# Two-layer model on one core: keys, values and router of layer 1 in three equal pieces, and products summed over tokens on DVE

## Chip, cores and metric

The program runs on one core of one Trainium2 chip. The metric is the device time in microseconds (us) of one execution of the whole program; of the kernel before there are three runs without a profiler, and one profiled execution.

## The reference

Two layers, each an attention part and a feed-forward part, over 4096 tokens of 512 numbers. This change is in the attention part of layer 1, which is no softmax attention: keys and values of a token are normed and multiplied number by number, and these products are summed over the 2048 tokens of a batch (the kernel has two batches). The second part cut out below is the router whose logits are made beside them.

```python
Xn = _layernorm(X, gamma, beta)
QKV = Xn @ W_in + b_in
Q, K, V = jnp.split(QKV, 3, axis=-1)
K = _rotary(K, ROT_DIM)
V = _rotary(V, ROT_DIM)
A = jnp.sum(_cos_sim(K) * _cos_sim(V), axis=-2)
A = (1.0 - IDENTITY_WEIGHT) * A + IDENTITY_WEIGHT
Y = A[:, None, :] * Q
Y = Y @ W_out + b_out
return Y + X
...
logits = x.astype(jnp.float32) @ router_weight.astype(jnp.float32).T
```

The last line is the router of layer 1; the kernel makes these logits (`logits1`, 8 columns) from the same transposed tile as keys and values. `axis=-2` is the axis of the tokens.

## The kernel before

The program is a row of stages, each with its own instruction streams for the five engines: front, attention, experts, the combining stage (`phase_mix`), and the last stage (`phase_last`). Engines are tied together by semaphores only; each runs its stream in the order in which it is written.

`phase_mix` runs from about 2350 to 3115 us. Its tokens are cut in 8 groups (`GROUPS`) of 4 tiles (`GT`) of 128 tokens, so 32 tiles, 16 for each batch. An outer loop has 10 iterations of 18 steps (`STEPS`). In iteration `it` the first 8 iterations do the shared expert of layer 0 for group `it`: in every step PE has twelve matmuls of 512 columns (`gate_up`, into `b_psG` or `b_psU`, or `down_of`, into `b_psY`). Between them stands the work on the groups before: a group `n` has a clock `rel`, which is `k` in iteration `n + 1` and `k + 18` in iteration `n + 2`. In iterations 8 and 9 only that work is left, and PE has nothing of its own to do between the pieces. This stretch, from 3016 us on, is called the stage's end here.

For group `n`: at `rel` 2 to 7 DVE adds up the layer's output (`sums`, `residual`) and works out the norm (`variance`, `deviation`). Tile `j` of the group then has its turn from `rel = 8 + 4 j`: PE transposes the normed tile into the PSUM bank `psX` (`turn`), ACT and DVE make of it the upper and the lower half of `c_xT` (`x_upper`, `x_lower`); two steps later PE does `router` (twelve matmuls of 8 columns into a corner of `psX`) and `keys(t, 0)` (twelve of 512 columns into `psK`), one step later `keys(t, 1)`. Twelve are three for each of the four chunks of 128 rows: `mm3` multiplies upper by lower, lower by upper, and upper by upper half. DVE takes each piece out of PSUM (line 2130 for the logits, line 2040 for `c_kv`), and PE's next piece into the same bank waits for that (`kv_ready`). One step later POOL turns keys and values by the table and multiplies them into `c_prod` (`rotate`, six operations), and ACT sums their squares. At `rel` 25 and 26 DVE makes the group's factors `rn` of them. At `rel` 29 PE does `similar`: sixteen fp32 matmuls of one column (they show as 32 in the trace), products as the stationary side and `rn` as the moving one, whose result (4 columns, in `psX`) DVE copies to `aparts` (line 2140). The last stage sums `aparts` over the four groups of a batch.

DVE's order inside a step matters: first the expert's product or half, then the group one iteration back, then the group two back. So the fourth tile of a group (`rel` 20 to 24, steps 2 to 6 of an iteration) meets the next group's `sums` and `residual` on DVE (steps 2 to 4), and stands behind them.

Of the kernel before, what the change touches and what calls it, by code (L numbers as in the profile page):

```python
# [20 lines left out]
P = 128  # L21
# [1456 lines left out]
def phase_mix(nc, env):  # L1478
# [13 lines left out]
    A_AT = 29  # L1492
    with ctx:
# [14 lines left out]
        wr = [sb(f"c_wr{h}", [P, KC, NROUTED], F32R) for h in range(2)]  # L1508
# [8 lines left out]
        rs = rsb[:, 0, :].rearrange("p (a i o) -> p a i o", a=2, o=2)  # L1517
        n2 = [sb(f"c_n2{i}", [P, GT, 2]) for i in range(2)]
# [16 lines left out]
        psL = psX[:, 0, 0:NROUTED]  # L1535
        psA = psX[:, 0, NROUTED:NROUTED + KC]
# [16 lines left out]
        rot, prod_ready, a_full, a_used = sem("c_rot"), sem("c_prod"), sem("c_a_full"), sem("c_a_used")  # L1553
        wr_in, wr_hi, wr_split = sem("c_wr_in"), sem("c_wr_hi"), sem("c_wr_split")
# [91 lines left out]
        def _(pool):  # L1646
            def rotate(t):
# [16 lines left out]
                if t >= GT:  # L1664

                    pool.wait_ge(a_full, t // GT)
# [36 lines left out]
        def _(pe):  # L1703
# [29 lines left out]
            def turn(t):  # L1733
# [6 lines left out]
                if t % GT == 1 and t > GT:  # L1740

                    pe.wait_ge(a_used, t // GT)
# [59 lines left out]
            for g, k, after in steps():  # L1802
# [9 lines left out]
                for n, rel in after:  # L1812
                    if (t := tile_at(n, rel, XS)) is not None:
                        turn(t)
                    if (t := tile_at(n, rel, XS + 2)) is not None:
                        router(t)
# [3 lines left out]
                    if rel == A_AT:  # L1820
                        similar(n)

        @block.scalar
        def _(act):
# [69 lines left out]
            def fold_upper(c):  # L1894
                act.wait_ge(centred, 2 * KC + c + 1)
                act.activation(env.wkv1[0][:, c, :, :], w[c][:, 1:3, :], ACT.Copy).then_inc(i_hi, 1)
# [5 lines left out]
            act.activation(wr[0][:, :, :], wr_raw[:, :, :], ACT.Copy).then_inc(wr_hi, 1)  # L1902
# [41 lines left out]
        def _(dve):  # L1944
# [85 lines left out]

            def keys(t, a):
                dve.wait_ge(k_full, 2 * t + a + 1)
                if t == a == 0:
                    dve.wait_ge(b_out, 3)
                if a == 0 and t % GT == 0:
                    dve.wait_ge(r2_ready, t // GT + 1)
                if a == 0 and t >= 2:
                    dve.wait_ge(prod_ready, t - 1)
                    dve.wait_ge(sq_ready, t - 1)
                dve.scalar_tensor_tensor(kv[t % 2][:, a, :], psK[:, :], env.stat[:, t, 2:3], env.bkv[:, a, :],  # L2040
                                         ALU.mult, ALU.add).then_inc(kv_ready, 1)
# [649 lines left out]
```

## Time and profile before

| what | us |
|---|---|
| runs without a profiler, median of 3 | 4430.65 (4429.25 to 4431.05) |
| profiled execution, first to last instruction | 4443.7 |
| PE busy (matmuls) | 4139.1, 93% |
| DVE busy | 2115.4, 48% |
| ACT busy | 1662.0, 37% |
| POOL busy | 1352.3, 30% |

The profiled execution is the one whose trace is read here. Its own time is the span of 4443.7 us; no other time of it is recorded, and it is 13 us longer than the median of the runs without a profiler. Busy shares are of the whole span.

### The profile page before, as it was taken

To read this page: it belongs to the slowest core of one execution; us is meant where nothing else is said; L and a number is where in the kernel's file an instruction comes from. 1 tells how busy PE (TensorE), PEld (TensorE's weight loads), DVE (VectorE), ACT (ScalarE), POOL (GpSimd) and SP (SyncE) were. 2 spreads that over 40 slices of the span, in tenths; PEclk is the share of its full clock that TensorE was granted. 3 is DMA by queue.
4 is the path that set the end of the run, shared out by engine and by line. 5 is a ranking of instruction groups with operands and counts; after the bars stand their busy time and mean duration, and the time that the engine had idled before them with its cause. 6 is when DMAs were issued, how large, how long until landed. Compare 5 with 4: busy or idle time off the path is not lost. (4 is left out here: it accounts for less than half of the span.)

```text
span 4443.7 us, 69429 instructions
## 1 busy us (share of the span) xinstructions
PE 4139.1 (93%) x23045; PEld 3550.2 (80%) x23046; DVE 2115.4 (48%) x4125; ACT 1662.0 (37%) x3234; POOL 1352.3 (30%) x2020
## 2 busy tenths in 40 slices
PE   6975999899999999999997999997899999999998
PEld 5864777689889999989985777785688888788887
DVE  4447888744444444444435445543343333333333
ACT  2214777634334444443433333331332222222222
POOL 0002454455555555555551333334000000000000
PEclk9877999999999999999998999997999999999999
DMA  5767787455556556555645444431432331231321
GB/s 189 282 239 192 137 162 143 97 136 123 113 120 129 128 124 136 121 128 117 154 75 181 152 140 145 154 105 50 152 107 71 100 102 60 100 102 60 102 81 45
DMA packets 351912, 561.41 MB, mean 126 GB/s; under 512 B 33089, under 2 KB 198625, under 8 KB 347490
## 3 DMA queue, kind: packets, MB, share of 16 engines
q1 hardware_dynamic: 282770, 394.19, 29.8%
q0 software_dynamic: 68944, 164.62, 17.3%
q8 instruction: 120, 1.97, 0.2%
q14 instruction: 78, 0.64, 0.1%
HBM read 384.36 MB, written 174.34 MB: 126 GB/s over the span
## 5 line engine op out<-in xcount | busy, mean ns | idle before, releaser
L1250 POOL DMA_INDIRECT acc_d<-e_yw,e_to x208 | 335.9, 1615 | 287.0 <-ACT e_yw L1407 270.4
L2310 POOL DMA_DIRECT2D out<-d_res x32 | 17.3, 542 | 1305.3 <-DVE d_res L2542 1305.3
L2489 DVE TENSOR_TENSOR d_h<-d_sg,d_psU 128x512 f32<-128x512 f32 x144 | 99.1, 688 | 521.3 <-PE d_psU L107 462.9
L983 ACT ACTIVATE a_pr<-a_sm,a_nmax 128x272 f32<-128x272 f32 x512 | 263.8, 516 | 124.9 <-DVE a_nmax L1037 120.7
L105 PE MATMUL e_psG<-e_gu,e_xT 128*128 128x352 f32 x832 | 290.6, 349 | 10.0 <-DVE e_xT L1461 9.2
L1469 DVE TENSOR_TENSOR e_h<-e_sg,e_psU 128x352 f32<-128x352 f32 x208 | 108.3, 521 | 396.4 <-ACT e_sg L1420 393.8
L107 PE MATMUL e_psG<-e_gu,e_xT 128*128 128x352 f32 x832 | 272.5, 327 | 0.0
L106 PE MATMUL e_psG<-e_gu,e_xT 128*128 128x352 f32 x832 | 272.3, 327 | 0.0
L105 PE MATMUL e_psU<-e_gu,e_xT 128*128 128x352 f32 x832 | 270.9, 326 | 0.0
L106 PE MATMUL e_psU<-e_gu,e_xT 128*128 128x352 f32 x832 | 269.5, 324 | 0.0
L105 PE MATMUL e_psY<-e_wd,e_hT 128*128 128x512 f32 (+1 forms) x624 | 265.7, 426 | 1.2 <-DVE e_hT L1452 1.2
L107 PE MATMUL e_psU<-e_gu,e_xT 128*128 128x352 f32 x832 | 266.4, 320 | 0.0
L1220 POOL DMA_INDIRECT e_xs<-xn_d,e_idx x209 | 209.9, 1004 | 174.4 <-POOL e_idx L1217 168.4
L2417 ACT ACTIVATE d_hT<-d_h 128x512 fp32r<-128x512 f32 x144 | 91.0, 632 | 459.6 <-DVE d_h L2489 401.6
L1037 DVE CUSTOM_DVE_ANT_0 a_sm<-a_psS,a_mask 128x272 f32<-128x272 f32 x512 | 214.2, 437 | 82.5 <-PE a_psS L877 54.4
L1420 ACT ACTIVATE e_sg<-e_psG 128x352 f32<-128x352 f32 x208 | 96.4, 463 | 409.5 <-PE e_psU L107 409.5
L107 PE MATMUL e_psY<-e_wd,e_hT 128*128 128x512 f32 (+1 forms) x624 | 247.1, 396 | 0.0
L106 PE MATMUL e_psY<-e_wd,e_hT 128*128 128x512 f32 (+1 forms) x624 | 245.4, 393 | 0.0
L2411 ACT ACTIVATE d_sg<-d_psG 128x512 f32<-128x512 f32 x144 | 86.0, 598 | 423.5 <-PE d_psG L107 423.4
L1401 ACT ACTIVATE e_hT<-e_psH 128x384 fp32r<-128x384 f32 x208 | 102.2, 491 | 372.6 <-PE e_psH L1340 372.6
L105 PE MATMUL d_psG<-d_x,d_gu 128*128 128x512 f32 x576 | 225.4, 391 | 12.7 <-DMA d_x<-xT_d 12.7
L105 PE MATMUL d_psU<-d_x,d_gu 128*128 128x512 f32 x576 | 227.8, 395 | 0.0
(430 smaller groups left out, 12004.9 us busy)
## 6 DMA issues: line engine op xcount, KB each, us to landing
d_gu_raw<-in_wgu SPq DMA_DIRECT2D x144, 512.0 KB, 3.3
qk_d<-f_qk SPq DMA_DIRECT2D x32, 1024.0 KB, 6.5
a_q<-qk_d SPq DMA_DIRECT2D x96, 256.0 KB
a_k<-qk_d SPq DMA_DIRECT2D x96, 256.0 KB, 4.7
e_rawgu<-in_w_gate SPq DMA_DIRECT2D x32, 704.0 KB, 5.9
e_rawgu<-in_w_up SPq DMA_DIRECT2D x32, 704.0 KB, 5.8
b_gu_raw<-in_wgu SPq DMA_DIRECT2D x40, 512.0 KB, 3.8
xT_d<-f_xT SPq DMA_DIRECT2D x16, 1024.0 KB, 14.3
```

Of the source, the lines that this page charges most:

```text
L105: pe.matmul(out, lhs[0], rhs[1], start=first, stop=False, **kw)
L106: pe.matmul(out, lhs[1], rhs[0], start=False, stop=False, **kw)
L107: return pe.matmul(out, lhs[0], rhs[0], start=False, stop=last, **kw)
L983: act.activation(pr[half][:, h % HH, :], sm[s % SR][:, :], ACT.Exp, bias=nmax[s % SR][:, :], scale=-1.0, accum_out=rs[u % 2][:, h:h + 1]). ...
L1037: dve.tensor_tensor_reduce(out=sm[s % SR][:, :], in0=psS[s % SR][:, PERSIST:2 * KW], in1=m[:, :], scale=-SCALE, scalar=3.0e38, op0=ALU.add ...
L1220: pool.indirect_dma_start(rows[:, :], None, env.xn_d, bass.IndirectOffsetOnAxis(ap=idx[k][:, :].bitcast(U32), axis=0))\
L1250: pool.indirect_dma_start(env.acc_d, bass.IndirectOffsetOnAxis(ap=to[:, :].bitcast(U32), axis=0), yw[:, :], None, compute_op=ALU.add).then ...
L1401: act.activation(hT[0][:, :, :], psH[:, :, :], ACT.Copy).then_inc(hT_hi, 1)
L1420: act.activation(sg[:, :], psG[:, 0:M], ACT.Silu).then_inc(sg_ready, 1)
L1469: dve.tensor_tensor(hv[:, :], sg[:, :], psU[:, 0:M], ALU.mult).then_inc(h_ready, 1)
L2417: act.activation(h2[q % 2][0][:, :], hv[q % 2][:, :], ACT.Copy).then_inc(h_hi, 1)
L2489: ins = dve.tensor_tensor(hv[q % 2][:, :], sg[q % 2][:, :], psU[:, :], ALU.mult)
```

## The change

Keys, values and router have 512 + 512 + 8 = 1032 columns. They are put side by side in one tensor (`wkv1`, 1032 columns for each chunk) and cut in three pieces of 344 (`CW`). The third piece (336 columns of values and the 8 of the router) comes first and goes into the whole bank `psX` (`last_keys`), the others into `psK` as before. DVE takes out three pieces of 336 or 344 columns where it took two of 512, and the logits as before.

The sum over tokens is moved: DVE adds the weighed products of each tile into one tile `simacc` (`add`, at `rel` 27 to 30), and PE turns this into a column once per batch with a column of ones, four matmuls in place of sixteen for each group (`similar`, at `rel` 31 of every fourth group, into `psK`). POOL's wait before it writes `c_prod` again is now for `added`, no longer for `a_full`. The sum over groups in the last stage falls away.

```diff
-    A_AT = 29
+    GB = GROUPS // B
+    ADD_AT = 27
+    A_AT = ADD_AT + GT
+    CW = (2 * D + NROUTED) // 3
...
+        simacc = rsb[:, 1, :]
...
-        psL = psX[:, 0, 0:NROUTED]
-        psA = psX[:, 0, NROUTED:NROUTED + KC]
+        psXf = psX[:, :, :].rearrange("p c k -> p (c k)")
+        psL = psXf[:, CW - NROUTED:CW]
+        psA = psK[:, 0:KC]
...
-                    pool.wait_ge(a_full, t // GT)
+                    pool.wait_ge(added, t - GT + 1)
...
-                if t % GT == 1 and t > GT:
-
-                    pe.wait_ge(a_used, t // GT)
...
-            def router(t):
+            def columns(t, out, a):
+
+                for c in range(KC):
+                    ins = mm3(pe, out, [xT[t % 2][h][:, c, :] for h in range(2)],
+                              [env.wkv1[h][:, c, a * CW:(a + 1) * CW] for h in range(2)], c == 0, c == KC - 1)
+                return ins
+
+            def last_keys(t):
                 pe.wait_ge(x_split, t + 1)
                 if t == 0:
                     pe.wait_ge(wr_split, 1)
-                for c in range(KC):
-                    ins = mm3(pe, psL, [xT[t % 2][h][:, c, :] for h in range(2)], [wr[h][:, c, :] for h in range(2)],
-                              c == 0, c == KC - 1)
-                ins.then_inc(l_full, 1)
+                    pe.wait_ge(i_split, KC)
+                columns(t, psXf[:, 0:CW], 2).then_inc(l_full, 1)
 
             def keys(t, a):
                 if t or a:
                     pe.wait_ge(kv_ready, 2 * t + a)
-                else:
-                    pe.wait_ge(i_split, KC)
+                if t == GT * GB + 1 and a == 0:
+
+                    pe.wait_ge(a_used, 1)
+                columns(t, psK[:, 0:CW], a).then_inc(k_full, 1)
+
+            def similar(b):
+                pe.wait_ge(added, GT * GB * (b + 1))
+
+                pe.wait_ge(kv_ready, 2 * min(GT * GB * (b + 1) + 1, TILES))
                 for c in range(KC):
-                    ins = mm3(pe, psK[:, :], [xT[t % 2][h][:, c, :] for h in range(2)],
-                              [env.wkv1[h][:, c, a, :] for h in range(2)], c == 0, c == KC - 1)
-                ins.then_inc(k_full, 1)
...
-                for c in range(KC):
-                    for j in range(GT):
-                        ins = pe.matmul(psA[:, c:c + 1], prod[:, j, c * P:(c + 1) * P], rn[g % 2][:, j:j + 1],
-                                        start=j == 0, stop=j == GT - 1)
+                    ins = pe.matmul(psA[:, c:c + 1], simacc[:, c * P:(c + 1) * P], ones[:, 0:1],
+                                    start=True, stop=True)
                 ins.then_inc(a_full, 1)
...
+            def last_keys(t):
+                dve.wait_ge(l_full, t + 1)
+                if t == 0:
+                    dve.wait_ge(b_out, 3)
+                if t % GT == 0:
+                    dve.wait_ge(r2_ready, t // GT + 1)
+                if t >= 2:
+                    dve.wait_ge(prod_ready, t - 1)
+                    dve.wait_ge(sq_ready, t - 1)
+                dve.tensor_copy(env.logits1[:, t, :], psL)
+                scaled(t, psXf[:, 0:CW - NROUTED], 2 * CW, 2 * D).then_inc(l_used, 1)
...
+            def add(t):
+                g, j = divmod(t, GT)
+                dve.wait_ge(rn_ready, g + 1)
+                dve.wait_ge(prod_ready, t + 1)
+                if t % (GT * GB) == 0:
+                    if t:
+                        dve.wait_ge(a_full, g // GB)
+                    dve.tensor_scalar(simacc[:, :], prod[:, j, :], rn[g % 2][:, j:j + 1], None, ALU.mult)\
+                       .then_inc(added, 1)
+                    return
+                dve.wait_ge(added, t)
+                dve.scalar_tensor_tensor(simacc[:, :], prod[:, j, :], rn[g % 2][:, j:j + 1], simacc[:, :],
+                                         ALU.mult, ALU.add).then_inc(added, 1)
```

The first place is DVE's stream at the fourth tile of a group, behind `residual` of the next group (`c_s`, `c_x`, `c_st`). Before:

```order
L1985 TENSOR_TENSOR c_s<-c_s,c_acc 128x512
L1987 TENSOR_TENSOR c_x<-c_s,c_x 128x512
L1989 BN_STATS c_st<-c_x 128x6
L2130 COPY logits<-c_psX 128x8
L2040 SCALAR_TENSOR_TENSOR c_kv<-c_psK,stat,bkv 128x512
L1970 TENSOR_TENSOR b_hT<-b_h,b_hT 128x512
L1950 TENSOR_TENSOR b_gu<-b_gu_raw,b_gu 128x1024
```

With the change one more operation stands there before PE's bank `psK` is free:

```order
L1991 TENSOR_TENSOR c_x<-c_s,c_x 128x512
L1993 BN_STATS c_st<-c_x 128x6
L2050 COPY logits<-c_psX 128x8
L2037 SCALAR_TENSOR_TENSOR c_kv<-c_psX,stat,bkv 128x336
L2037 SCALAR_TENSOR_TENSOR c_kv<-c_psK,stat,bkv 128x344
L1974 TENSOR_TENSOR b_hT<-b_h,b_hT 128x512
L1954 TENSOR_TENSOR b_gu<-b_gu_raw,b_gu 128x1024
```

The two pieces of 512 columns have become three, of which two lie side by side here.

The second place is also on DVE, in steps 8 to 12 of an iteration, where the group two back gives its factors `c_rn` (first row) and, with the change, its products are added into `c_rs`. With the change:

```order
L2012 TENSOR_TENSOR c_rn<-c_rn,c_tmp_n 128x4
L2064 TENSOR_SCALAR c_rs<-c_prod,c_rn 128x512
L1969 TENSOR_TENSOR b_h<-b_sg,b_psU 128x512
L2050 COPY logits<-c_psX 128x8
L2037 SCALAR_TENSOR_TENSOR c_kv<-c_psX,stat,bkv 128x336
L2037 SCALAR_TENSOR_TENSOR c_kv<-c_psK,stat,bkv 128x344
L2068 SCALAR_TENSOR_TENSOR c_rs<-c_prod,c_rn,c_rs 128x512
L1974 TENSOR_TENSOR b_hT<-b_h,b_hT 128x512
L1954 TENSOR_TENSOR b_gu<-b_gu_raw,b_gu 128x512
L2037 SCALAR_TENSOR_TENSOR c_kv<-c_psK,stat,bkv 128x344
L2068 SCALAR_TENSOR_TENSOR c_rs<-c_prod,c_rn,c_rs 128x512
L2032 TENSOR_TENSOR c_xT<-c_psX,c_xT 128x512
```

Before, no `c_rs` row was there, and in step 11 DVE's copy of the column (line 2140) waited for PE. The three shown here and a fourth in step 12 stand among the pieces of the tile whose turn it is.

The third place is on PE, at the end of `keys(t, 1)` in step 11 of the iteration (`c_psK` is the piece, `b_psG` the expert's next matmuls). Before:

```order
L105 MATMUL c_psK<-wkv,c_xT 128x512
L106 MATMUL c_psK<-wkv,c_xT 128x512
L107 MATMUL c_psK<-wkv,c_xT 128x512
L1773 MATMUL c_psX<-c_rn,c_prod 128x1 x16
L105 MATMUL b_psG<-b_x,b_gu 128x512
L106 MATMUL b_psG<-b_x,b_gu 128x512
```

With the change:

```order
L105 MATMUL c_psK<-wkv,c_xT 128x344
L106 MATMUL c_psK<-wkv,c_xT 128x344
L107 MATMUL c_psK<-wkv,c_xT 128x344
L105 MATMUL b_psG<-b_x,b_gu 128x512
L106 MATMUL b_psG<-b_x,b_gu 128x512
```

The sixteen one-column matmuls are gone from here, in all eight groups; four of them per batch come back at `rel` 31.

## Rows read from the trace of the kernel before

**Rows 1.** The page's head
```profile
span 4443.7 us, 69429 instructions
```

**Rows 2.** Windows: stretch; length; busy PE, PEld, DVE, ACT, POOL; PEclk; DMA
```profile
2543.00:2630.70 87.70, 86.14 (x409) 70.08 (x408) 43.27 (x76) 30.27 (x53) 31.24 (x37) 0.96 0.41 141
...
2630.70:2716.90 86.20, 84.63 (x409) 68.73 (x408) 43.30 (x76) 30.27 (x53) 31.24 (x37) 0.98 0.42 144
...
3016.30:3114.10 97.80, 69.09 (x277) 55.82 (x276) 33.99 (x70) 17.65 (x42) 41.20 (x51) 0.75 0.13 49
...
2545.50:2552.30 6.80, 6.80 (x22) 5.74 (x23) 0.16 (x1) 0.00 (x0) 4.56 (x6) 0.50 0.09 39
```

**Rows 3.** Timeline of PE, one tile: start, length, instruction
```profile
2644.56 0.17 PE L105 MATMUL c_psX<-c_wr,c_xT 128*128 128x8 f32 x1
...
2645.82 0.47 PE L105 MATMUL c_psK<-wkv,c_xT 128*128 128x512 f32 x1
...
2648.69 0.39 PE L105 MATMUL b_psG<-b_x,b_gu 128*64 128x512 f32 x1
...
2651.46 0.40 PE L105 MATMUL c_psK<-wkv,c_xT 128*128 128x512 f32 x1
...
2654.25 0.39 PE L105 MATMUL b_psU<-b_x,b_gu 128*64 128x512 f32 x1
```

**Rows 4.** Timeline of PE in the experts' stage, pieces of 352 columns
```profile
1499.78 0.32 PE L106 MATMUL e_psG<-e_gu,e_xT 128*128 128x352 f32 x1
...
1502.85 0.32 PE L107 MATMUL e_psU<-e_gu,e_xT 128*128 128x352 f32 x1
```

**Rows 5.** Timeline of PE, the products summed over tokens
```profile
2542.96 4.55 PE L1773 MATMUL c_psX<-c_rn,c_prod 128*128 128x1 f32 x32
...
2630.73 3.66 PE L1773 MATMUL c_psX<-c_rn,c_prod 128*128 128x1 f32 x32
...
2634.25 0.78 PE L105 MATMUL b_psG<-b_x,b_gu 128*128 128x512 f32 x1
```

**Rows 6.** Groups by form, DVE: busy us, mean ns, idle before
```profile
L2040 DVE SCALAR_TENSOR_TENSOR c_kv<-c_psK,stat,bkv 128x512 f32<-128x512 f32 x64 | 48.0, 750 | 171.7 <-PE c_psK L107 171.7
...
L2058 DVE SCALAR_TENSOR_TENSOR c_acc<-c_rs,i_beta,c_acc 128x1536 f32<-128x1536 f32 x1 | 1.8, 1821 | 0.1
```

**Rows 7.** Waits of PE, 2430 to 3010 us
```profile
PE c_psK L105 <- DVE c_kv L2040: 9.4, 6, 1.6
```

**Rows 8.** Timeline around the wait for a tile's keys
```profile
2603.19 0.15 DVE L2130 COPY logits<-c_psX 128x8 f32<-128x8 f32 x1
...
2604.05 0.50 PE L105 MATMUL c_psK<-wkv,c_xT 128*128 128x512 f32 x1 [1.56 <-DVE c_kv L2040]
```

**Rows 9.** Waits, timeline and window of PE in the experts' stage
```profile
PE e_psH L1340 <- DVE e_h L1469: 10.2, 5, 2.3
...
1200.83 0.90 PE L1340 MATMUL e_psH<-ident,e_h 128*128 128x128 f32 x3 [2.09 <-DVE e_h L1469]
...
1200.60:1204.00 3.40, 3.17 (x12) 3.05 (x13) 1.93 (x4) 1.21 (x2) 1.71 (x4) 0.50 0.38 66
```

**Rows 10.** Timeline of the stage's end
```profile
3063.74 0.37 PE L105 MATMUL c_psX<-c_wr,c_xT 128*128 128x8 f32 x1 [1.41 <-DVE c_xT L2028]
...
3066.32 0.77 PE L105 MATMUL c_psK<-wkv,c_xT 128*128 128x512 f32 x1
...
3072.37 0.50 PE L105 MATMUL c_psK<-wkv,c_xT 128*128 128x512 f32 x1 [0.84 <-DVE c_kv L2040]
...
3106.96 6.98 PE L1773 MATMUL c_psX<-c_rn,c_prod 128*128 128x1 f32 x32 [6.54 <-POOL c_prod L1669]
...
3113.98 0.16 DVE L2140 COPY aparts<-c_psX 128x4 f32<-128x4 f32 x1 [7.74 <-PE c_psX L1773]
```

**Rows 11.** Timeline of DVE, one operation twice
```profile
2587.90 2.32 DVE L1950 TENSOR_TENSOR b_gu<-b_gu_raw,b_gu 128x1024 fp32r<-128x1024 f32 x1
...
2604.51 1.22 DVE L1950 TENSOR_TENSOR b_gu<-b_gu_raw,b_gu 128x1024 fp32r<-128x1024 f32 x1
```

More of the change, by code:

```diff
@@ L1507, in phase_mix @@
         xT = [[sb(f"c_xT{i}{h}", [P, KC, P], F32R) for h in range(2)] for i in range(2)]
-        wr = [sb(f"c_wr{h}", [P, KC, NROUTED], F32R) for h in range(2)]
         wr_raw = sb("c_wr_raw", [P, KC, NROUTED])
@@ L1553, in phase_mix @@
         rot, prod_ready, a_full, a_used = sem("c_rot"), sem("c_prod"), sem("c_a_full"), sem("c_a_used")
+        added = sem("c_added")
         wr_in, wr_hi, wr_split = sem("c_wr_in"), sem("c_wr_hi"), sem("c_wr_split")
@@ L1815, in _ @@
                     if (t := tile_at(n, rel, XS + 2)) is not None:
-                        router(t)
+                        last_keys(t)
                         keys(t, 0)
@@ L1819, in _ @@
                         keys(t, 1)
-                    if rel == A_AT:
-                        similar(n)
+                    if rel == A_AT and n % GB == GB - 1:
+                        similar(n // GB)
         @block.scalar
@@ L1895, in fold_upper @@
                 act.wait_ge(centred, 2 * KC + c + 1)
-                act.activation(env.wkv1[0][:, c, :, :], w[c][:, 1:3, :], ACT.Copy).then_inc(i_hi, 1)
+                act.activation(env.wkv1[0][:, c, 0:2 * D].rearrange("p (a n) -> p a n", a=2), w[c][:, 1:3, :], ACT.Copy)\
+                   .then_inc(i_hi, 1)
             gu_upper(0)
@@ L1901, in _ @@
             act.wait_ge(wr_in, 16)
-            act.activation(wr[0][:, :, :], wr_raw[:, :, :], ACT.Copy).then_inc(wr_hi, 1)
+            act.activation(env.wkv1[0][:, :, 2 * D:3 * CW], wr_raw[:, :, :], ACT.Copy).then_inc(wr_hi, 1)
             for g, k, after in steps():
@@ L2029, in x_lower, with scaled @@
                    .then_inc(x_split, 1)
+            def scaled(t, out, lo, hi):
+                return dve.scalar_tensor_tensor(
+                    kv[t % 2].rearrange("p a n -> p (a n)")[:, lo:hi], out, env.stat[:, t, 2:3],
+                    env.bkv[:, :, :].rearrange("p a n -> p (a n)")[:, lo:hi], ALU.mult, ALU.add)
+            def last_keys(t):
[9 more added lines that the diff above has]
+                scaled(t, psXf[:, 0:CW - NROUTED], 2 * CW, 2 * D).then_inc(l_used, 1)
             def keys(t, a):
                 dve.wait_ge(k_full, 2 * t + a + 1)
[L2033 to L2041, printed above, removed]
+                scaled(t, psK[:, 0:CW], a * CW, (a + 1) * CW).then_inc(kv_ready, 1)
+            def add(t):
[11 more added lines that the diff above has]
+                                         ALU.mult, ALU.add).then_inc(added, 1)
             def norms(g):
@@ L2067, in fold_lower @@
                 dve.wait_ge(i_hi, k + 1)
-                dve.tensor_tensor(env.wkv1[1][:, k, :, :], w[k][:, 1:3, :], f(env.wkv1[0][:, k, :, :]), ALU.subtract)\
-                   .then_inc(i_split, 1)
+                upper, lower = (env.wkv1[h][:, k, 0:2 * D].rearrange("p (a n) -> p a n", a=2) for h in range(2))
+                dve.tensor_tensor(lower, w[k][:, 1:3, :], f(upper), ALU.subtract).then_inc(i_split, 1)
             def fold(k):
@@ L2098, in _ @@
             dve.wait_ge(wr_hi, 1)
-            dve.tensor_tensor(wr[1][:, :, :], wr_raw[:, :, :], f(wr[0][:, :, :]), ALU.subtract).then_inc(wr_split, 1)
+            dve.tensor_tensor(env.wkv1[1][:, :, 2 * D:3 * CW], wr_raw[:, :, :], f(env.wkv1[0][:, :, 2 * D:3 * CW]),
+                              ALU.subtract).then_inc(wr_split, 1)
             for g, k, after in steps():
@@ L2128, in _ @@
                     if (t := tile_at(n, rel, XS + 2)) is not None:
-                        dve.wait_ge(l_full, t + 1)
-                        dve.tensor_copy(env.logits1[:, t, :], psL).then_inc(l_used, 1)
+                        last_keys(t)
                         keys(t, 0)
@@ L2137, in _ @@
                         over_norms(n)
-                    if rel == A_AT:
-                        dve.wait_ge(a_full, n + 1)
-                        dve.tensor_copy(env.aparts[:, n, :], psA).then_inc(a_used, 1)
+                    if ADD_AT <= rel < ADD_AT + GT:
+                        add(GT * n + rel - ADD_AT)
+                    if rel == A_AT and n % GB == GB - 1:
+                        dve.wait_ge(a_full, n // GB + 1)
+                        dve.tensor_copy(env.aparts[:, n // GB, :], psA).then_inc(a_used, 1)
 def phase_last(nc, env):
@@ L2501, in similarity @@
             def similarity():
-                do(dve.tensor_reduce(a[:, :, :], env.aparts[:, :, :].rearrange("p (b t) k -> p b k t", b=B), AX.X, ALU.add))
-                do(dve.tensor_scalar(a[:, :, :], a[:, :, :], 0.5, 0.5, ALU.mult, ALU.add))
+                do(dve.tensor_scalar(a[:, :, :], env.aparts[:, :, :], 0.5, 0.5, ALU.mult, ALU.add))
             def scale(b):
@@ L2601, in program @@
         env.stat = sb("stat", [P, TILES, 3])
-        env.aparts = sb("aparts", [P, GROUPS, KC])
+        env.aparts = sb("aparts", [P, B, KC])
         env.logits1 = sb("logits1", [P, TILES, NROUTED])
@@ L2627, in program @@
                 sb0 = lambda name, shape, dt=F32: similar.enter_context(nc.sbuf_tensor(name, shape, dt))
-                env.wkv1 = [sb0(f"wkv1{h}", [P, KC, 2, D], F32R) for h in range(2)]
+                env.wkv1 = [sb0(f"wkv1{h}", [P, KC, 2 * D + NROUTED], F32R) for h in range(2)]
                 env.bkv = sb0("bkv", [P, 2, D])
```

4 lines of the change are left out of this document (removed).

## Prediction

> **What bounds the kernel now.** I read the page's head first, then busy time by stretches, then PE's timeline of one tile, then PE's waits, then DVE around them. The profiled execution spans 4443.7 us [rows 1], 13.05 us above the median of the runs shown, 4430.65. The sum below is a difference within the trace; I take it off both, 4443.7 for a profiled run and 4430.65 for the forecast.
>
> The change touches the combining stage alone. Of its two stretches by groups, 87.7 and 86.2 us long, PE is busy 86.14 and 84.63, DVE only 43.3, ACT 30.3, POOL 31.2 [rows 2]. What PE lacks is 1.56 us in each, and that is one wait: 9.4 us in six times, all for DVE's keys [rows 7]. So up to 3016 us the stage lasts as long as PE's list of matmuls, and what leaves that list comes off the end. After 3016 us PE is busy 69 of 98 us, at a granted clock of 0.75 [rows 2]: a chain PE, ACT, DVE, PE again.
>
> The granted clock is 0.96 and 0.98 in those groups, where nearly all of PE's time is matmuls of 512 columns. Windows over the other groups read 0.96 and 0.98 by turns, six in all. The fall stands in the same place each time: at the end of the one-column matmuls of `similar`. In the first group they run 4.55 us from 2542.96, and from 2545.5 to 2552.3 the clock is at 0.50, the 1.2 GHz level [rows 2, 5]. In the second they take 3.52 us at full clock (2630.73 to 2634.25), and the next matmul already lasts 0.78 [rows 5].
>
> **The change, part by part.** *Pieces.* One tile now: the router's twelve take 2645.82 - 2644.56 = 1.26 us, `keys(t, 0)` 2648.69 - 2645.82 = 2.87, `keys(t, 1)` 2654.25 - 2651.46 = 2.79 [rows 3]; together 6.92 us for 36 matmuls and 1032 columns. The router's matmuls start 0.105 us apart for 8 columns: they pay for their number, not for their columns. The change keeps 36 matmuls and the same columns, evenly. No matmul of 344 columns is in the trace. From above: 512 columns start 2.79 / 12 = 0.2325 apart; less 168 columns at 2.4 GHz (0.070) that is 0.163. From below: 352 columns start (1502.85 - 1499.78) / 19 = 0.1616 apart [rows 4]; less 8 columns, 0.158. I take 0.160, since both are near: 36 x 0.160 = 5.76 us, 1.16 less per tile, 37.1 us for 32 tiles (33.7 to 39.4 at the bounds).
>
> The Trainium skill has a rule for this gap (page "TensorE: Matmul & The Clock Gate", section "Back-to-back issue gap"): N / 2.4 + 2.5 ns for a matmul alone. By it a piece would take 0.146 us, a tile 5.25, and the pieces would bring 53 us in place of 37. The same rule gives 0.149 for 352 columns, where the row has 0.1616, so the trace does not agree and the row decides.
>
> *Products.* `similar` goes from eight places. Seven run at full clock, 3.5 us each by the row [rows 5]: 24.6 us. The one of the first batch comes back with 8 of the 32 passes, 0.9 us: 23.7 us saved. The eighth is at the stage's end, below.
>
> *Clock.* With `similar` gone, the six falls lose their cause. At half clock PE does half its work: 0.04 x 87.7 = 3.5 us, then 0.02 x 86.2 = 1.7, three times each (0.5 x 6.8 = 3.4 by the window itself [rows 2]): 15.4 us. The eight passes left take 0.9 us, less than the router's 1.26 us of short matmuls [rows 3], behind which no fall stands.
>
> *The wait grows.* At the fourth tile of a group PE waits 1.56 us for DVE, whose queue is full of `residual`: copy of the logits at 2603.19, then one eviction, then PE at 2604.05 [rows 8]. The order of the changed kernel has two evictions there. 512 columns take 750 ns and 1536 take 1821, so a column is 1.05 ns [rows 6] and a piece of 344 or 336 about 0.57 us; DVE overlaps some 0.07 of two neighbours (the copy began 0.07 before the eviction would, by the 0.86 us between copy and PE). Two pieces: 0.57 + 0.50 = 1.07 for 0.75, PE's bank is free 0.32 later. PE also comes sooner: 3.84 for two pieces against 1.26 + 2.87 = 4.13, 0.29. The wait becomes 1.56 + 0.32 + 0.29 = 2.17 us. The whole 0.61 is lost, six times: 3.7 us. (If DVE's `sums` start earlier by the shorter eviction before them, 0.17 less.) Behind this eviction on DVE stand `b_hT`, `b_gu` and the norm; for them wait PE's `down_of` and `gate_up` of later steps and the transposes of step 8; the stream of PE has a step of 2.7 us or more in between, so 0.3 us there costs nothing.
>
> *Does that wait lower the clock?* In the experts' stage PE waits five times for `e_h`, 10.2 us in all, longest 2.3 [rows 9]; one is 1.59 and no fall follows, the other four are 2.09 to 2.31 and each is followed by one: 2.09 before 1200.83, and 0.50 from 1200.6 to 1204.0 [rows 9]. Six waits of 1.56 in our stage have none. 2.17 is in the group of those that have, so I take a fall of 3.4 us, 1.7 us lost, six times: 10.2 us back. Against it: behind those four waits stand short transposes, here full matmuls. Both ends: nothing, and 6 x 3.4 = 20.4 us if each is as long as the fall at 2545.5.
>
> *Adds.* 31 SCALAR_TENSOR_TENSOR of 512 columns at about 0.75 us [rows 6] and one or two TENSOR_SCALAR, 24 us of DVE time, 3 us per group on an engine that idles 44. Cover: in steps 9 to 12 DVE waits for PE (for the keys alone 171.7 us in the stage [rows 6]), and it no longer waits for `similar`. Queued behind an add are evictions: PE needs a bank back one step of 2.7 us later, so even an add doubled in length stays hidden. Without the cover an add would cost its 0.75, 24 us in all. Products and factors are there: tile 3's product is begun at `rel` 24, needed at 30. POOL's new wait is for an add one step or more before it.
>
> POOL and DVE do slow each other. The same `b_gu` operation takes 1.22 us alone and 2.32 beside POOL [rows 11]. The Trainium skill says why (page "SBUF — State Buffer", section "SBUF: two separate sides"): the pair of ports that the two share is locked for a whole instruction, and DVE operations with two SBUF inputs are among those that need it. The adds are such; by the row an add beside POOL would be 1.1 us longer, which the cover above still holds.
>
> *Stage's end.* The last `similar` runs from 3106.96 to 3113.98, at half clock [rows 10]. Now the factors are ready shortly before the last product, so of four adds (0.69 each, overlapped) I take three behind 3106.96, 2.1 us, and then eight passes at half clock, 6.98 / 4 = 1.75: the end is at 3110.9, 3.1 sooner. The five tiles of the chain get their 1.16 above as if at full clock. At half clock the first two pieces take (3072.37 - 0.84) - 3063.74 = 7.8 us [rows 10]; 24 pieces at 344 / 1.2 GHz = 0.287 plus the 0.017 that 0.160 holds over 0.143 take 7.3: a gain of 0.5 where full clock has 0.29, so little more. The wait of 0.84 behind them [rows 10] shrinks with the eviction by 0.18, five times, 0.9. With the same gain at the eviction ahead of the norm and of the last squares I put 1.9 us for all this. Together 5.0; both ends 0 and 8.
>
> *Sum.* 37.1 + 23.7 + 15.4 - 3.7 - 10.2 + 5.0 = 67.3 us. 4430.65 - 67.3 = 4363.4 (profiled 4376).
>
> **Rivals.**
> A, the forecast: the wait grows and the clock falls behind it, 4363; by itself 4354 to 4372 (the bounds of a piece -2.3 and +3.4, and three long falls of six +5).
> B, the wait grows and the clock stays: 10.2 less, 4353. For it: full matmuls on both sides of the wait. Against it: four of four.
> C, DVE becomes late in more places or all falls are long. Price: 6 x 1.7 = 10.2 for long falls, or 1 us more per group from adds in front of evictions, with the stage's end not shortened: 4374 to 4384. For it: DVE's full queue in steps 2 to 6. Against it: DVE idle half of each group.
> D, slower: a piece of 344 columns, which begins at no multiple of a round number of bytes in `wkv1`, does not run at its columns' rate. Everything but the pieces brings 67.3 - 37.1 = 30.2 us; 1152 matmuls take 221.4 us now, so the change turns slower from (221.4 + 30.2) / 1152 = 0.218 us for one. If each costs a full bank's 0.2325: 268 - 221.4 = 46 more, less 30: 4447. Against it: 352 columns in the experts' stage, also cut from a longer row, show 0.1616.
> E, the skill's gap of 0.146 for a piece: 16 us less than A, 4347; the row of 352 columns speaks against it.
> F, no effect, because something else ends last: PE's 98% busy speaks against it.
>
> **How the numbers follow.** A 0.50, B 0.27, C 0.14, D 0.04, E 0.03, F 0.02. Forecast A, 4363. The range reaches to B below (4353, with the lower bound of a piece 4347) and to the near part of C above: 4346 to 4379, which leaves D, F and half of C and E out. A change of over 0.2%, 9 us, is about what can be told from none. Faster: A, B, C, E, 0.94; same: F, 0.02; slower: D, 0.04.
>
> **What would show it.** PE's pieces of 344 columns start 0.158 to 0.163 apart. The windows of groups are 77 to 79 us long. One wait of 1.9 to 2.3 us for `c_kv` per group, in six groups, and behind it matmuls of 512 columns of 0.63 for 3.4 us; none behind `keys(t, 1)` in step 11. DVE's adds near 0.75 us, no wait of PE for `added` but at the end. The copy to `aparts` about 4 us behind the last product. Wrong it would be made by waits of PE at other tiles, by falls that stay where `similar` was, or by pieces above 0.17.

## The result, and the profile after

The changed kernel takes 4356.1 us (median of four runs, 4351.0 to 4358.9), the kernel before 4430.9 (four runs, 4429.3 to 4436.9): a ratio of 0.9827, 95% interval 0.9815 to 0.9839 (the two medians alone give 0.9831), 74.7 us less. The forecast was 4363.4, so 67.3 less. A second set of five runs (experiment 5) gave 0.9822.

The page's head of after and its busy times:

```profile
span 4354.7 us, 69033 instructions
...
PE 4047.8 (93%) x22805; PEld 3499.5 (80%) x22806; DVE 2142.3 (49%) x4182; ACT 1661.1 (38%) x3234; POOL 1359.5 (31%) x2020
```

PE (TensorE, the matmul engine) is as busy in share as before, with 91 us less work; DVE (VectorE) has 27 us more. The two profiled spans are 89.0 us apart [rows 1], the medians 74.7. Of those 89, 7 lie ahead of the stage (the experts' stage ends at 2327.4, before at 2334.1, with work that the change does not touch). So a difference read in the two traces is some us too large, and the medians decide.

Windows of after over three groups and the one fall in them, then the stage's end, then its last three tiles but one piece (columns as in [rows 2]; a "fall" is a stretch in which the granted clock of PE is 0.50, the lower of its two levels):

```profile
2503.10:2579.70 76.60, 74.58 (x377) 63.40 (x376) 46.52 (x84) 30.25 (x53) 32.31 (x37) 1.00 0.48 162
2579.70:2656.30 76.60, 74.59 (x376) 63.41 (x376) 46.75 (x84) 30.25 (x53) 32.16 (x37) 1.00 0.48 162
2656.30:2734.40 78.10, 76.09 (x376) 64.88 (x376) 46.75 (x84) 30.25 (x53) 32.16 (x37) 0.98 0.46 159
...
2658.70:2662.10 3.40, 3.40 (x14) 3.30 (x13) 1.97 (x8) 1.49 (x2) 0.00 (x0) 0.50 0.92 298
2950.40:3024.10 73.70, 41.84 (x205) 38.43 (x204) 39.53 (x80) 17.65 (x42) 39.44 (x49) 0.77 0.18 64
2983.60:3012.70 29.10, 22.09 (x133) 20.16 (x132) 10.34 (x19) 6.16 (x16) 21.75 (x26) 1.00 0.20 69
```

A group lasted 87.7 or 86.2 us [rows 2] and now lasts 76.6, or 78.1 where the clock falls. PE lacks 2.0 us in each, DVE is busy 46.5 where it was 43.3: the adds are there, and PE does not lose by them.

Timeline of PE, the pieces of one tile with what stands ahead of and behind them, then the next group's wait:

```profile
2649.60 0.32 PE L105 MATMUL c_psX<-wkv,c_xT 128*128 128x344 f32 x1
...
2651.48 0.32 PE L105 MATMUL c_psK<-wkv,c_xT 128*128 128x344 f32 x1
...
2653.39 0.39 PE L105 MATMUL b_psY<-b_wd,b_hT 128*128 128x512 f32 x1
...
2658.31 0.42 PE L105 MATMUL c_psK<-wkv,c_xT 128*128 128x344 f32 x1 [2.02 <-DVE c_kv L2037]
2658.58 0.40 PE L106 MATMUL c_psK<-wkv,c_xT 128*128 128x344 f32 x1
...
2659.63 0.49 PE L107 MATMUL c_psK<-wkv,c_xT 128*128 128x344 f32 x1
```

Twelve matmuls of 344 columns take 1.88 and 1.91 us, so they start 0.157 and 0.159 apart; a tile has about 5.69 us of them where it had 6.92. Behind the wait the matmuls last 0.49 instead of 0.32, up to 2662.1: that is the fall of the window above.

PE's waits from 2430 to 2940 us, which answers to [rows 7]:

```profile
PE c_psK L105 <- DVE c_kv L2037: 12.1, 6, 2.0
PE c_psX L1746 <- ACT c_xn L1866: 0.6, 1, 0.6
```

Six waits of 2.02 us, one for each group, and none for an add. Two of the six have a fall behind them (at 2658.7 and 2737.2, 3.4 us each), four have none.

DVE's groups by form, 2420 to 3060 us (busy, mean ns of one, idle before):

```profile
L2037 DVE SCALAR_TENSOR_TENSOR c_kv<-c_psK,stat,bkv 128x344 f32<-128x344 f32 x64 | 36.8, 575 | 100.7 <-PE c_psK L107 100.6
L2068 DVE SCALAR_TENSOR_TENSOR c_rs<-c_prod,c_rn,c_rs 128x512 f32<-128x512 f32 x30 | 27.2, 907 | 0.6
...
L2037 DVE SCALAR_TENSOR_TENSOR c_kv<-c_psX,stat,bkv 128x336 f32<-128x336 f32 x32 | 17.8, 557 | 0.0
```

An eviction takes 575 or 557 ns, an add 907 in the mean. Two adds of one group show what is in this mean, with POOL's (GpSimd's) operations beside them:

```profile
2606.99 0.74 DVE L2068 SCALAR_TENSOR_TENSOR c_rs<-c_prod,c_rn,c_rs 128x512 f32<-128x512 f32 x1
2607.22 1.67 POOL L1659 TENSOR_TENSOR c_sq<-c_kv,c_trig 128x512 f32<-128x512 f32 x1 [10.34 <-issue]
...
2610.41 0.69 DVE L2032 TENSOR_TENSOR c_xT<-c_psX,c_xT 128x512 fp32r<-128x512 f32 x1 [2.68 <-ACT c_xT L1874]
2610.59 1.29 POOL L1667 TENSOR_TENSOR c_sq<-c_sq,c_rs 128x512 f32<-128x512 f32 x1
2611.02 1.40 DVE L2068 SCALAR_TENSOR_TENSOR c_rs<-c_prod,c_rn,c_rs 128x512 f32<-128x512 f32 x1
```

The add that begins 0.23 us ahead of POOL's operation takes 0.74 us; the one that begins inside POOL's takes 1.40. Queued behind the second on DVE is `b_h` of the expert (next start 2612.53), and PE waits for nothing of it.

The stage's end on the timeline, as in [rows 10]:

```profile
3017.70 0.64 DVE L2012 TENSOR_TENSOR c_rn<-c_rn,c_tmp_n 128x4 f32<-128x4 f32 x1
3018.28 0.72 POOL L1674 TENSOR_TENSOR c_prod<-c_sq 128x256 f32<-128x256 f32 x1
3018.37 3.83 DVE L2068 SCALAR_TENSOR_TENSOR c_rs<-c_prod,c_rn,c_rs 128x512 f32<-128x512 f32 x4
3022.25 1.87 PE L1776 MATMUL c_psK<-i_ones,c_rs 128*128 128x1 f32 x8 [9.56 <-DVE c_rs L2068]
3024.16 0.16 DVE L2170 COPY aparts<-c_psK 128x4 f32<-128x4 f32 x1 [1.96 <-PE c_psK L1776]
```

The factors are ready at 3018.3, the last product at 3019.0. All four adds stand behind the factors, 3.83 us of them, where three (2.1 us) were forecast behind the last product; the eight passes take 1.87. The copy is 5.2 us behind the last product, before 7.0 [rows 10], forecast about 4.

### The profile page after: what moved, and what is told of

It is laid out like the page before. It is cut to its first block and busy times, and to the rows that moved or that the text cites. A ratio compares the mean times of both kernels' runs of the same rounds, so it can differ in the third digit from the quotient of the medians.

```text
span 4354.7 us, 69033 instructions
## 1 busy us (share of the span) xinstructions
PE 4047.8 (93%) x22805; PEld 3499.5 (80%) x22806; DVE 2142.3 (49%) x4182; ACT 1661.1 (38%) x3234; POOL 1359.5 (31%) x2020
## 5 line engine op out<-in xcount | busy, mean ns | idle before, releaser
L1037 DVE CUSTOM_DVE_ANT_0 a_sm<-a_psS,a_mask 128x272 f32<-128x272 f32 x512 | 213.9, 436 | 82.2 <-PE a_psS L877 54.2
L105 PE MATMUL d_psG<-d_x,d_gu 128*128 128x512 f32 x576 | 225.2, 391 | 13.7 <-DMA d_x<-xT_d 13.0
```

The lines of the kernel that those rows point to most:

```text
L105: pe.matmul(out, lhs[0], rhs[1], start=first, stop=False, **kw)
L1037: dve.tensor_tensor_reduce(out=sm[s % SR][:, :], in0=psS[s % SR][:, PERSIST:2 * KW], in1=m[:, :], scale=-SCALE, scalar=3.0e38, op0=ALU.add ...
```

## Experiments

The theory after the result: PE's list is still the bound; its pieces and its one-column matmuls are what got shorter; the clock fell at the one-column matmuls, and falls behind a wait only sometimes; the adds are hidden. Rivals: the halves of the change need each other, or the falls have nothing to do with the one-column matmuls, or DVE's adds cost something that the shorter list hides. Experiments 1 to 4 share one set of runs of the kernel before (4430.2 us), 5 to 8 another (4432.1). In the first set the changed kernel did not run; where experiments 3 and 4 are held against it, that is its 4356.1 us from the result above.

**1. The pieces alone.** The three pieces of 344 as in the change, the sum over tokens by `similar` on PE as before.

```diff
-        psA = psK[:, 0:KC]
+        psA = psXf[:, CW:CW + KC]
...
                 for c in range(KC):
-                    ins = pe.matmul(psA[:, c:c + 1], simacc[:, c * P:(c + 1) * P], ones[:, 0:1],
-                                    start=True, stop=True)
+                    for j in range(GT):
+                        ins = pe.matmul(psA[:, c:c + 1], prod[:, j, c * P:(c + 1) * P], rn[g % 2][:, j:j + 1],
+                                        start=j == 0, stop=j == GT - 1)
```

> The change with only its first half: three pieces of 344 columns, but the sum over tokens as before, sixteen one-column matmuls per group at rel 29 (their result stands in the columns of the bank psX behind the third piece). Theory: the two halves add up. A tile took 6.92 us and takes 5.69 in the trace of the change, so 1.23 x 32 = 39 us less; the wait for the fourth tile's keys grows by 0.46 us, six times, 3 us; the falls of the clock stay behind similar, six of them, 15 us of them as before. Time about 4395 (ratio 0.992). Rival: the pieces of 344 columns load PE less evenly and the falls get longer or more: 4405 and above, with more than six stretches of 1.2 GHz before the stage's end.

Measured: 4392.5 us, ratio 0.9914 (0.9898 to 0.9931), 37.6 less than before. Its list of PE's waits, 2430 to 2960 us, first row:

```profile
PE c_psK L105 <- DVE c_kv L2034: 12.1, 6, 2.0
```

The longer wait comes with the pieces and needs nothing of the adds. Two of the six have a fall behind them, and three more falls stand where `similar` is. Six had been expected there, as in the kernel before, so not every run of the short matmuls has one.

**2. The sum on DVE alone.** The adds and one column for each batch as in the change; keys and values in two pieces of 512 columns, the router's twelve of 8 as before (the columns of `similar` stand in the corner of `psX` here).

```diff
-                columns(t, psXf[:, 0:CW], 2).then_inc(l_full, 1)
+                for c in range(KC):
+                    ins = mm3(pe, psL, [xT[t % 2][h][:, c, :] for h in range(2)], [wr[h][:, c, :] for h in range(2)],
+                              c == 0, c == KC - 1)
+                ins.then_inc(l_full, 1)
...
-                columns(t, psK[:, 0:CW], a).then_inc(k_full, 1)
+                for c in range(KC):
+                    ins = mm3(pe, psK[:, :], [xT[t % 2][h][:, c, :] for h in range(2)],
+                              [env.wkv1[h][:, c, a, :] for h in range(2)], c == 0, c == KC - 1)
+                ins.then_inc(k_full, 1)
```

> The change with only its second half: router and keys as before (8 and 512 columns), the products summed over tokens by DVE and turned into a column once per batch (its result in the corner of psX). Theory: 7 x 3.5 - 0.9 = 24 us of matmuls, 15 us of falls, and some 2 us at the end: time about 4390 (ratio 0.991), the groups' windows at a granted clock of 1.00, PE's wait for the fourth tile's keys at 1.56 as before. Rival: the falls had to do with DVE's wait for similar or with the router's short matmuls: then the clock stays at 0.96 to 0.98 and the time is about 4405.

Measured: 4387.9 us, ratio 0.9905 (0.9889 to 0.9922), 42.2 less. Windows over two of its groups, and its waits of PE from 2430 to 2960 us:

```profile
2502.80:2583.80 81.00, 79.45 (x376) 64.03 (x376) 46.33 (x80) 30.24 (x53) 32.32 (x37) 1.00 0.45 153
2583.80:2664.80 81.00, 79.41 (x377) 64.02 (x376) 46.58 (x80) 30.25 (x53) 32.17 (x37) 1.00 0.45 153
...
PE c_psK L105 <- DVE c_kv L2041: 9.5, 6, 1.6
```

81.0 us is before's 86.2 [rows 2] less 3.5 of one-column matmuls and less 1.7 of a fall, and before's 87.7 less 3.5 and 3.4, to within 0.2. The waits are those of before, and no group has a fall: all six falls of before have gone with `similar`. The two halves add up: 0.0086 and 0.0095 of the time apart make 0.0181, together they bring 0.0173 or 0.0178, a difference well inside the intervals. Neither needs the other.

**3. Short matmuls put back.** The change, and for the first six groups the sixteen one-column matmuls at `rel` 29 again, into columns of `psX` that nothing reads. POOL's next products wait for them, as for `similar` before.

```diff
+            def short(g):
+                pe.wait_ge(prod_ready, GT * (g + 1))
+                pe.wait_ge(rn_ready, g + 1)
+                pe.wait_ge(l_used, GT * (g + 1) + 1)
+                for c in range(KC):
+                    for j in range(GT):
+                        ins = pe.matmul(psXf[:, CW + c:CW + c + 1], prod[:, j, c * P:(c + 1) * P], rn[g % 2][:, j:j + 1],
+                                        start=j == 0, stop=j == GT - 1)
+                ins.then_inc(short_done, 1)
...
+                    if rel == 29 and n < GROUPS - 2:
+                        short(n)
```

> The whole change, and beside it the sixteen one-column matmuls per group again at rel 29, for the first six groups; nobody reads their result, DVE does not wait for them, only POOL waits before it writes the products again. Theory: the short matmuls themselves lower the clock: each of the six groups is 3.5 us longer by them and a fall of 3.4 or 6.8 us stands at their end, 1.7 or 3.4 us lost: about +21 +15 = 4392 (ratio 0.991). Rival: it was DVE's wait, or chance of position: +21 alone, 4377.

Measured: 4386.1 us (4380.8 to 4393.5), ratio 0.9894 (0.9878 to 0.9911), 30.0 above the changed kernel. Timeline of PE at one of them, and the window of its group:

```profile
2692.74 4.74 PE L1789 MATMUL c_psX<-c_rn,c_prod 128*128 128x1 f32 x32
2697.34 0.77 PE L105 MATMUL b_psG<-b_x,b_gu 128*128 128x512 f32 x1
2697.91 0.63 PE L106 MATMUL b_psG<-b_x,b_gu 128*128 128x512 f32 x1
...
2666.80:2751.70 84.90, 82.87 (x409) 71.00 (x410) 46.20 (x84) 30.15 (x53) 31.63 (x37) 0.94 0.42 146
```

4392 was expected, and 4377 by the rival that the short matmuls cost only their own time; the measured time lies between. The time of the matmuls alone is 6 x 3.5 = 21 us. The other 9 us are put down to the clock by what the trace shows, which is that of the slowest of the four runs (4393.5 us): four of the six runs of short matmuls have a fall that begins inside them and lasts 6.8 us, the first two have none. So the falls come with this kind of work, put in by itself, but not with every piece of it. With it five of the six waits of 2.02 have a fall behind them, where the changed kernel has two. In the trace that makes 4 x 3.4 + 3 x 1.7 = 18.7 us on top of the 21. Two of those five stand ahead of the first fall at short matmuls (2585.8 and 2667.7, before 2695.0), so it is not one fall that brings the other.

**4. Adds twice.** The change, and every add done twice, the first time into a piece of scratch.

```diff
                 dve.wait_ge(added, t)
+                dve.scalar_tensor_tensor(scratch, prod[:, j, :], rn[g % 2][:, j:j + 1], simacc[:, :],
+                                         ALU.mult, ALU.add)
                 dve.scalar_tensor_tensor(simacc[:, :], prod[:, j, :], rn[g % 2][:, j:j + 1], simacc[:, :],
                                          ALU.mult, ALU.add).then_inc(added, 1)
```

> The whole change with every add done twice on DVE, the first time into a tile that nobody reads (30 more SCALAR_TENSOR_TENSOR of 512 columns, 0.75 to 1.4 us each, 27 us in all). Theory: the adds lie in DVE's waits for PE, so the groups' windows stay at 76.6 us; only at the stage's end three or four of them lie on the path, 2 to 4 us: about 4359 (ratio 0.984). Rival: DVE is near its limit in steps 9 to 12, with POOL on the shared ports: 10 to 27 us more, and new waits of PE for c_xT or c_kv.

Measured: 4366.1 us, ratio 0.9859 (0.9842 to 0.9875), 10 above the changed kernel and 7 above what was expected: a miss. Windows over two of its groups and its stage's end:

```profile
2504.50:2581.10 76.60, 74.58 (x377) 63.40 (x376) 50.30 (x87) 30.26 (x53) 33.24 (x37) 1.00 0.47 162
2581.10:2659.30 78.20, 76.18 (x377) 64.75 (x376) 51.34 (x88) 30.14 (x53) 33.06 (x37) 0.98 0.46 158
...
2956.60:3033.60 77.00, 41.34 (x205) 37.91 (x204) 46.03 (x88) 17.66 (x42) 40.24 (x49) 0.81 0.18 62
```

The first group lasts 76.6 us, as without the doubling, with 4 us more of DVE's work: in the groups an add is hidden. Of the 10 us, 8.3 can be placed elsewhere: the stage's end is 77.0 for 73.7 (the last adds stand in the chain, 2.7, and one wait for `c_xT` is 1.7 longer in it), the column of the first batch now waits 1.63 us (PE for the last add), and four waits of six have a fall in this profile, where after's has two (3.4 us more). The last is chance or a cause of its own; these runs do not tell which.

**5. The changed kernel again**, to be compared with the next three on the same chip.

> The changed kernel once more, as it is, to be compared with the three beside it. 4352 to 4359. Of PE's six waits of 2.02 us for the fourth tile's keys, 0 to 6 have a fall of the clock behind them: two had in its first trace, two in the kernel with the pieces alone, four with the adds doubled, five with the short matmuls back; none of the twelve waits of 1.56 to 1.59 in the kernel before and with the sums alone had one. If that is the rule, the number changes from run to run and with it the time, by 1.7 us for each.

Measured: 4354.3 us (4352.5 to 4358.7), ratio 0.9822 (0.9809 to 0.9836), 77.9 less than before. Again two falls behind the six waits, and behind the same two, the third and the fourth. The number had been expected to change from run to run; in these two profiles it did not.

**6. The bank of the keys first.** DVE takes the keys out of `psK` before the logits and the piece in `psX`.

```diff
                     dve.wait_ge(sq_ready, t - 1)
+                dve.wait_ge(k_full, 2 * t + 1)
+                scaled(t, psK[:, 0:CW], 0, CW).then_inc(kv_ready, 1)
                 dve.tensor_copy(env.logits1[:, t, :], psL)
                 scaled(t, psXf[:, 0:CW - NROUTED], 2 * CW, 2 * D).then_inc(l_used, 1)
...
                         last_keys(t)
-                        keys(t, 0)
```

> The changed kernel, but at each tile DVE first takes the piece out of psK, for which PE waits, and then the logits and the third piece out of psX. Theory: the wait at the fourth tile shrinks by one eviction and the copy, 0.57 us, to about 1.45, six times, and no fall of the clock follows any more (nearest rows: 1.56, none in twelve): 3.4 + 1.7 x 2 to 4 = 7 to 10 us less, about 4348. Rival: the falls come from the place, not from the wait's length, and stay: 3.4 us less, and two or more falls behind waits of 1.45.

Measured: 4346.3 us, ratio 0.9802 (0.9788 to 0.9815), 8.0 below experiment 5. First row of its waits, 2430 to 2940 us (the seventh, 0.8 us, is in the stage's end), and one group:

```profile
PE c_psK L105 <- DVE c_kv L2037: 9.6, 7, 1.5
...
2579.10:2655.10 76.00, 74.54 (x376) 63.40 (x376) 46.39 (x84) 30.25 (x53) 32.16 (x37) 1.00 0.48 163
...
2943.80:3014.70 70.90, 38.87 (x204) 35.62 (x204) 39.07 (x80) 17.66 (x42) 39.34 (x49) 0.82 0.19 67
```

Six waits of 1.48, no fall in any group. 6 x 0.6 by the windows and 2 x 1.7 for the falls are 7.0. The stage's end is shorter too in this profile (second window), 70.9 for 73.7 us, at a granted clock of 0.82 for 0.77. The sum, 9.8, is more than the 8.0 of the medians; the runs of this kernel spread from 4342 to 4348.

**7. No wait.** In step 4 DVE takes out the fourth tile's pieces before it does the next group's last two `residual`. Nothing is left out; the two are only later.

```diff
-                    if rel in (3, 4):
-                        residual(GT * n + 2 * (rel - 3))
-                        residual(GT * n + 2 * (rel - 3) + 1)
+                    if rel == 3:
+                        residual(GT * n)
+                        residual(GT * n + 1)
...
+                for n, rel in after:
+                    if rel == 4:
+                        residual(GT * n + 2)
+                        residual(GT * n + 3)
```

> The changed kernel, but in step 4 DVE does the evictions of the fourth tile of the group before first, and two of the four residual pieces of the next group behind them. Theory: the wait of 2.02 us is DVE's queue and nothing else, so it goes, six times, with the falls behind it and most of the wait of 3.04 at the stage's end: 12 + 5 + 2 = 19 us less, about 4337. The norm comes out at about the same time, since DVE waits at most 1 us for PE's piece in between. Rival: the norm comes later, and PE waits for c_xn in front of the transposes in step 8 instead: 5 us less or nothing.

Measured: 4334.6 us (4331.4 to 4336.9), ratio 0.9777 (0.9764 to 0.979), 19.6 below experiment 5. This is the best kernel of the study. The first transpose of a group and that of the next on PE's timeline, windows over 370 us and over the stage's end, all of PE's waits from 2430 to 2925 us, and one wait in the stage's end:

```profile
2587.37 0.60 PE L1746 MATMUL c_psX<-ident,c_xn 128*128 128x128 f32 x4
...
2661.69 0.60 PE L1746 MATMUL c_psX<-ident,c_xn 128*128 128x128 f32 x4
...
2500.00:2870.00 370.00, 369.95 (x1872) 315.18 (x1871) 229.82 (x411) 151.26 (x265) 161.26 (x185) 1.00 0.47 161
2933.80:3004.10 70.30, 38.44 (x204) 35.20 (x204) 39.57 (x80) 17.66 (x42) 39.42 (x49) 0.84 0.20 67
...
PE c_psX L1746 <- ACT c_xn L1866: 1.5, 1, 1.5
...
2953.13 1.11 PE L1746 MATMUL c_psX<-ident,c_xn 128*128 128x128 f32 x4 [7.12 <-ACT c_xn L1866]
```

For 370 us PE is never idle and the clock never falls. A group is 2661.69 - 2587.37 = 74.3 us, where it was 76.6: the waits of 2.02 cost 2.3 each, 6 x 2.3 = 13.7 unrounded, and 2 x 1.7 for the falls make 17.1. The stage's end gives the rest: 70.3 us for 73.7. It does so not by its waits: the one of 3.03 us for `psK` in experiment 5's end has shrunk to 0.67, but the norm comes later and PE waits 7.12 us for it where it waited 4.74. The granted clock there is 0.84 for 0.77. The sum, 20.5, is 0.9 above the 19.6 of the medians.

**8. A longer wait.** The change, and at the fourth tile of each group one more eviction of 336 columns, into scratch, ahead of the copy of the logits.

```diff
+                if t % GT == GT - 1:
+                    dve.scalar_tensor_tensor(scratch[:, 0:336], psXf[:, 0:336], env.stat[:, t, 2:3], env.bkv[:, 0, 0:336],
+                                             ALU.mult, ALU.add)
                 dve.tensor_copy(env.logits1[:, t, :], psL)
```

> The changed kernel with one more eviction of 336 columns into a tile that nobody reads, in front of the logits' copy at the fourth tile of each group: it lengthens the wait by about 0.50 us, to 2.5. Theory: +3.0 us by the waits, +0.5 at the end, and a fall behind nearly each of the six in place of two or four: +3 to +7, in all 4362 to 4367. Rival: length does not matter: +3.5 alone, 4360, and half of the waits with a fall as before.

Measured: 4361.7 us (4358.1 to 4367.2), ratio 0.9841 (0.9828 to 0.9855), 7.5 above experiment 5. First row of its waits, and the window of one fall:

```profile
PE c_psK L105 <- DVE c_kv L2038: 15.0, 6, 2.5
...
2581.30:2584.70 3.40, 3.40 (x13) 3.21 (x12) 2.22 (x9) 1.49 (x2) 0.13 (x1) 0.50 0.79 261
```

Six waits of 2.50, four falls of 3.4 us. 6 x 0.5 for the waits and 2 x 1.7 for two more falls are 6.4 of the 7.5. A fall behind nearly each of the six had been expected; longer waits did not bring that.

## Why the prediction was right, and where it was off

The direction, the forecast's range and the place of the gain were right; the time is 7 us (74.7 for 67.3) below the forecast, by the second set of runs 10.6. By the prediction's own terms:

- **Pieces, 37.1 us.** 0.157 to 0.159 us for one instead of 0.160. A group of the sums alone lasts 81.0 us with a wait of 1.58, one of the change 76.6 with 2.02; so four tiles save 4.4 + 0.44 = 4.84, 1.21 each, 38.7 for 32. The bound of 0.158 from the 352-column row was the better one. The rule of the Trainium skill (page "TensorE: Matmul & The Clock Gate", section "Back-to-back issue gap") gave 0.146. The section gives it for a matmul by itself and says that in a stream of weight loads and matmuls both set the spacing; these pieces are such a stream and start 0.157 to 0.159 apart, so rival E is out.
- **Products and clock, 23.7 and 15.4 us.** Right. Experiment 2 shows both together in two windows, and in it no fall is left in any group. Experiment 3 shows that falls come with the short matmuls, at four of six; in experiment 1 it is three of six.
- **The wait grows, 3.7 us.** It became 2.02, not 2.17: six times 0.46 is 2.8 us.
- **The clock behind the wait, 10.2 us.** This is the step that failed. It said that 2.17 "is in the group of those that have" a fall, and took one for all six waits; there were two, 3.4 us in place of 10.2. Each fall had the size forecast (3.4 us, 1.7 lost). The "four of four" were waits of one stage in one execution. The trace of after has the same stage, which the change does not touch, and there the rule does not hold. Two of its waits, and a window behind each:

```profile
1978.55 0.55 PE L1340 MATMUL e_psH<-ident,e_h 128*128 128x128 f32 x3 [1.55 <-DVE e_h L1469]
...
2242.52 0.55 PE L1340 MATMUL e_psH<-ident,e_h 128*128 128x128 f32 x3 [1.95 <-DVE e_h L1469]
...
1979.40:1982.80 3.40, 3.06 (x10) 3.09 (x11) 0.85 (x2) 2.16 (x3) 1.44 (x3) 0.50 0.45 112
...
2242.50:2249.00 6.50, 6.18 (x37) 5.71 (x38) 4.25 (x6) 3.52 (x5) 4.24 (x8) 1.00 0.43 79
```

The shorter wait, 1.55 (with a second one of 0.64 at 1979.74), has a fall; the longer, 1.95, has none. So the rows gave a chance, and it was taken for certain. Rival B, with no fall at all, was nearer, in falls (0 against 3.4 us, where the forecast had 10.2) and in time (4353 against 4356.1, where the forecast had 4363.4). Over all kernels of the study, behind this one wait:

| wait, us | kernels (numbers are experiments) | falls |
|---|---|---|
| 1.48 | 6 | 0 of 6 |
| 1.56 to 1.59 | before, 2 | 0 of 12 |
| 2.02 | after, 1, 3, 4, 5 | 2, 2, 5, 4, 2 of 6 |
| 2.50 | 8 | 4 of 6 |

So it is 15 of 30 at 2.02 us. In this one place the share rises from none at 1.59 and below; that the length is the reason is not shown, and the two waits above speak against a simple limit. What decides which of six equal waits has one is open.

- **Adds, nothing.** Right in the groups (experiment 4's first window). Not so at the end: the prediction counted three adds of 0.69 behind the last product, and it was four of 0.96 behind the factors, which came as late as the product; the copy is 1.8 us sooner relative to the last product, not 3.1. One wait of the end was not in the sum at all: the first one for `psK` there grew from 1.59 us to 3.04.
- **The stage's end, 5.0 us.** Settled only in part. From PE's first wait there for a normed tile to PE's last matmul it lasts 94.0 us before (3019.9 to 3113.9), 82.2 with the pieces alone, 81.4 with the sums alone, 73.7 after. That is 20.3 less, where the terms that lie there sum to 14.3 (five tiles of 1.16, one `similar` of 3.5, and the 5.0). But the medians leave no room for these 6 us: 67.3 with the pieces at 38.7, the wait at 2.8 and the falls at 3.4 is 76.6, and 74.7 and 77.9 were measured. Most of the 6 us is clock in before's profile. The same 80 matmuls of two tiles in the end, first before, then with the sums alone, whose pieces are those of before:

```profile
3072.30:3097.30 25.00, 20.47 (x80) 15.94 (x80) 4.74 (x9) 3.63 (x10) 13.66 (x17) 0.80 0.12 45
...
3020.10:3040.40 20.30, 15.78 (x80) 12.39 (x80) 4.72 (x8) 3.63 (x10) 13.27 (x18) 1.00 0.20 73
```

At a granted clock of 0.80 they take 4.7 us longer. The short matmuls of `similar` need not be the reason: experiment 1 keeps them, and its clock is 1.00 in the same two tiles (3029.7 to 3047.2). Before's profile is 13 us above the median of its runs, as much as the 6 us here and the 7 ahead of the stage. So that one execution is the likely reason; with one profile of before, how often it is so is not known, and what the change gives in the end was not measured apart from that.

No rival with another sign showed: 344 columns run at their columns' rate (D), PE had no wait at another tile of the groups (C), and the change had its effect (F).

## What to carry to other kernels

When PE's list is the bound, few short matmuls can cost more than they last: look at the granted clock right behind them, and at whether an engine with idle time can take the sum instead. A wait that is left in it costs its length and a little more (2.3 us for 2.02) and now and then a fall of the clock, so after a change that shortens the list read the list of waits again: here moving two `residual` on DVE was worth 19.6 us more, a quarter of what the whole change brought. And a rule made of four events in one stage is a chance; put it into the sum as that. What a wait costs is read from the period of the groups, from one landmark to the same landmark in the next group.

## What was not expected of the hardware

- A wait of PE costs 0.2 to 0.3 us more than the idle time in its row: groups are 74.3 us without one, 76.0 with 1.48, 76.6 with 2.02 and 77.1 with 2.50 (experiments 7, 6, after, 8). The timeline of after shows where it lies. The last matmul before the wait starts at 2655.91 and lasts 0.39 in its row, and the next starts at 2658.31, 2.40 later, where neighbours are 0.23 apart: 2.17 lost. The one behind that is 0.27 later where they are 0.157: 0.11 more. Together 2.28 us, the 2.3 of the groups. The row counts idle time from the end of the last matmul, 0.16 after the next could have started.
- The same wait at the same place, six times in one execution, is followed by a fall of the clock sometimes and sometimes not; two profiles of the changed kernel have it at the same two of the six. The falls behind it are all 3.4 us long and those at one-column matmuls 3.4 or 6.8.
- An add of 512 columns that begins while an operation of POOL runs takes 1.40 us instead of 0.74 (1.40 or 1.41 in six groups of six). It is the order that counts: the add that begins 0.23 us ahead of POOL's operation keeps its 0.74, and POOL's takes 1.67 us there, where the median of the same operation is 1.31. `b_gu` shows the first case too [rows 11]. The Trainium skill's page "SBUF — State Buffer", section "SBUF: two separate sides", says that of the two engines whichever starts first holds a shared pair of ports for its whole instruction and the other is shut out; the rows agree with it, with 1.9 times the length here.
